# Three programs behind the rotary attention joined into one, with batch 0 a step ahead at both edges

## The reference

```
x = x + cross_attention_rotary(norm(x), ctx)      # 16 heads of 64, 2048 context rows
x = x + self_attention_0(norm(x))                 # 16 heads of 32, causal, rotary
x = x + norm(x) @ sign(weight).T
x = x + relu(cross_attention_1(norm(x), ctx) @ wo_w.T + wo_b)   # 16 heads of 32
x = x + self_attention_1(norm(x))                 # 16 heads of 64, causal
x = x + experts(norm(x))
# experts: scores = n @ Wr + br; the best 2 of 8 get softmax weights r[t, e]
# h = gelu(n @ W1[e] + b1[e]) (512 -> 2048); y = h @ W2[e] + b2[e]; out = sum_e r[t, e] * y
```

## Time and profile before

| what | value |
|---|---|
| median of 3 runs | 1226.79 us (1225.6 to 1227.8) |
| the profiled execution's own time | 1224.32 us |
| its span in the profile | 1222.2 us |
| PE busy | 1189.2 us (97%) |
| PE's weight loads busy | 954.2 us (78%) |
| DVE, ACT, POOL busy | 679.2, 531.7, 216.4 us |
| second cross-attention, first query projection to end | about 600 to 762 us |
| self-attention 1 | 762 to 840 us |
| experts | 840 to 1218 us |

### The profile page before, as it was taken

How to read it: one execution, slowest core, us unless ns; L and a number is a source line. 1 busy time by engine, 2 the same in 40 slices (tenths; PEclk the granted TensorE clock), 3 DMA queues, 4 the chain that set the end, 5 groups by cost and what they waited for, 6 DMA issues and landing times. The chain is left out here.

```text
span 1222.2 us, 23053 instructions
## 1 busy us (share of the span) xinstructions
PE 1189.2 (97%) x9712; PEld 954.2 (78%) x9712; DVE 679.2 (56%) x1210; ACT 531.7 (44%) x897; POOL 216.4 (18%) x178
## 2 busy tenths in 40 slices
PE   7999999999999999999899999997999999999998
PEld 6788888888788888865456676864989999999997
DVE  4654544545464534365788873044665665665662
ACT  5432333332333332214389994153644544444441
POOL 2243333434333433350000000010000000000000
PEclk9999999999999999999999999898999999999999
DMA  7210101010100020326313323301544554454440
GB/s 295 69 53 1 65 2 53 1 49 5 36 19 1 27 70 2 131 86 242 136 73 139 139 75 138 134 1 38 204 177 171 205 202 164 184 206 184 166 165 18
DMA packets 28157, 126.01 MB, mean 103 GB/s; under 512 B 2715, under 2 KB 2971, under 8 KB 17572
## 3 DMA queue, kind: packets, MB, share of 16 engines
q1 hardware_dynamic: 28068, 124.74, 27.2%
HBM read 124.20 MB, written 0.52 MB: 102 GB/s over the span
## 5 line engine op out<-in xcount | busy, mean ns | idle before, releaser
L566 POOL TENSOR_TENSOR norm_both<-norm_both,prob 128x512 f32<-128x512 f32 x118 | 154.8, 1312 | 149.2 <-DVE prob L358 141.8
L57 PE MATMUL mo_h_ps<-mo_x_hi,mo_w_hi 128*128 128x256 f32 x512 | 146.7, 286 | 2.1 <-DVE mo_x_lo L1800 2.1
L495 ACT ACTIVATE prob<-u_ps 128x512 f32<-128x512 f32 x128 | 66.1, 606 | 186.4 <-PE u_ps L668 186.4
L58 PE MATMUL mo_h_ps<-mo_x_lo,mo_w_hi 128*128 128x256 f32 x512 | 146.4, 286 | 0.0
L59 PE MATMUL mo_h_ps<-mo_x_hi,mo_w_lo 128*128 128x256 f32 x512 | 146.3, 286 | 0.0
L341 DVE TENSOR_TENSOR turned<-k_ps,tabs 128x512 f32<-128x512 f32 x32 | 22.1, 690 | 195.9 <-PE k_ps L59 195.9
L1754 DVE TENSOR_TENSOR mo_w_lo<-w_raw,mo_w_hi 128x2048 fp32r<-128x2048 f32 x32 | 73.3, 2292 | 73.8 <-ACT mo_w_hi L1703 73.8
L57 PE MATMUL k_ps<-ctx_hi,wk_hi 128*128 128x512 f32 x256 | 104.2, 407 | 0.0
L57 PE MATMUL u_ps<-wv_hi,ctx_hi 128*128 128x512 f32 x256 | 103.1, 403 | 0.8 <-ACT prob L495 0.8
L57 PEld LDWEIGHTS mo_h_ps<-mo_x_hi,mo_w_hi 128*128 128x128 f32 x512 | 99.8, 195 | 3.7 <-DVE mo_x_lo L1800 2.5
L484 ACT ACTIVATE vals<-u_ps 128x512 f32<-128x512 f32 x64 | 38.2, 597 | 145.8 <-PE u_ps L59 145.8
(11 more groups left out here) (264 smaller groups left out, 2297.6 us busy)
## 6 DMA issues: line engine op xcount, KB each, us to landing
w_raw<-in_w SPq DMA_DIRECT2D x64, 1024.0 KB, 6.3
ctx_raw<-in_ctx_rows SPq DMA_DIRECT2D x8, 1024.0 KB, 5.7
x_k<-in_ctx_T SPq DMA_DIRECT2D x8, 1024.0 KB, 7.0
x_val<-in_ctx_heads SPq DMA_DIRECT2D x8, 1024.0 KB, 4.9
tabs<-in_rot_tabs SPq DMA_DIRECT2D x8, 512.0 KB, 4.2
vals<-in_wq_rows SPq DMA_DIRECT2D x4, 512.0 KB, 8.0
...
x_mask<-in_mask SPq DMA_DIRECT2D x2, 1024.0 KB, 9.0
```

Source lines behind the costliest of these rows:

```text
L57: pe.matmul(out, w_hi, x_hi, start=start, stop=False)
L58: pe.matmul(out, w_hi, x_lo, start=False, stop=False)
L495: act.activation(prob[:, t % 2, i, :], u_ps[:, i, :], ACT.Exp).then_inc(s["exped"], 1)
L566: ins = pool.tensor_tensor(to, to, src, ALU.add)
```

## The change

`middle`, `self_attention` and `experts` become one function `latents` with one block; PSUM keeps its two groups of four banks, `bk[0]` and `bk[1]`, through all stages. The norms behind the second cross-attention and behind self-attention 1 are made for one batch at a time:

- `add(0)` and `moments(6, 0)` move to DVE's step t = 35 and `centred(6, 0)` to t = 36; ACT takes the root with its table load at t = 35; PE transposes batch 0 at t = 37.
- `project_cols1` works on one batch: four groups (queries and keys, batch 0 and 1) of 32 fp32 matmuls of 128 columns. The first half of the first group stands ahead of `project(1, (KD - 1,))`, the second half behind it, ahead of the transposes of batch 1.
- At the second edge the transposes of batch 0 stand ahead of the last two slices of `project_out1(1, ...)`.
- `hidden(0, 0)` is replaced by `hidden_plain`: for each batch 16 fp32 matmuls of 128 columns on the raw weights, so that unit needs no rounding (`high1(0, 0)` and `low1(0, 0)` are gone).
- `high1(0, 1)`, `high2(0, 0)`, `low1(0, 1)` and `low2(0, 0)` move ahead of the edge, into self-attention 1. For this `w2_lo` is placed elsewhere, off the output weights of that attention.
- SP fetches units 0 and 1 behind `x["y"]`, and unit 2 only after all of `hidden_plain` (`mo["h_mm"]` at 4), since that reads the raw place which unit 2 takes.

The other helpers are carried over with new names.

```diff
-    middle(nc, I, env)
-    self_attention(nc, I, env)
-    experts(nc, I, env)
+    latents(nc, I, env)
...
+        def held(m, b):
+
+            return bk[1 - (m ^ b)][:, 2 * m:2 * m + 2, :]
...
+            sp.wait_ge(x["y"], NB)
+            for U in range(2):
+                for raw, name, got in ((env["w1_raw"], "w1", env["w1_in"]), (env["w2_raw"], "w2", env["w2_in"])):
+                    sp.dma_start(raw[:, U, :, :], I[name][U * P:(U + 1) * P, :]
+                                 .rearrange("p (k n) -> p k n", k=4)).then_inc(got[U], 16)
...
+            sp.wait_ge(mo["h_mm"], NP)
+            for j in (2, 3):
+                load(0, j)
+            with sp.Fori(1, E) as e:
+                for j in range(NU):
+                    load(e, j)
...
+            def turn_norm(j, b, side, bank):
+                    ins = pe.transpose(bk[side][:, bank, k * P:(k + 1) * P], normed[:, b, k * P:(k + 1) * P], ident[:])
...
+            def project_cols1(m, b, ns):
+
+                pe.wait_ge(s["T_out"], 7 + b)
+                for n in ns:
+                    for k in range(KD):
+                        ins = pe.matmul(held(m, b)[:, n // 4, (n % 4) * P:(n % 4 + 1) * P],
+                                        (wq1, wk1)[m][:, k, n * P:(n + 1) * P], normed_T[:, k, b * P:(b + 1) * P],
+                                        start=(k == 0), stop=(k == KD - 1))
+                    if n % 4 == 3:
+                        ins.then_inc(a1["qkT"], 1)
...
+                pe.wait_ge(a1["qkT_out"], 6 + 2 * b)
...
+            def hidden_plain(b, ns):
+
+                pe.wait_ge(s1[0], 16)
+                pe.wait_ge(s["T_out"], 9 + b)
+                for n in ns:
+                    for k in range(KD):
+                        ins = pe.matmul(h_ps[:, n // 2, (n % 2) * TOK + b * P:(n % 2) * TOK + (b + 1) * P],
+                                        w1_raw[:, 0, k, n * P:(n + 1) * P], normed_T[:, k, b * P:(b + 1) * P],
+                                        start=(k == 0), stop=(k == KD - 1))
+                    if b == 1:
+                        ins.then_inc(mo["h_mm"], 1)
...
+                pe.wait_ge(mo["x_lo"], b + 1)
...
+                if t == NST + LAG - 2:
+                    turn_norm(6, 0, 0, 0)
                 if t == NST + LAG - 1:
                     project(1, range(KD - 1))
+            pe.wait_ge(w_in1, 16 * 3)
+            project_cols1(0, 0, range(4))
             project(1, (KD - 1,))
+            project_cols1(0, 0, range(4, KA1))
+            turn_norm(7, 1, 1, 2)
+            project_cols1(1, 0, range(KA1))
+            project_cols1(0, 1, range(KA1))
+            project_cols1(1, 1, range(KA1))
+            scores1(0)
...
+            project_out1(1, range(6))
+            turn_norm(8, 0, 1, 2)
+            project_out1(1, (6, 7))
+            hidden_plain(0, range(3))
+            turn_norm(9, 1, 1, 3)
+            hidden_plain(0, (3,))
+            hidden_plain(1, range(NP))
+            logits(0)
+            logits(1)
+            hidden(0, 1, first=True)
+            output(0, 0, 0, first=True)
+            hidden(0, 2)
+            turn_weights()
+            output(0, 1, 0, first=True)
+            hidden(0, 3)
...
+                if t == NST + 3:
+                    root(6, 0)
+            keep_cols1(0, 0, 0)
+            root(7, 1)
+            keep_cols1(0, 0, 1)
+            keep_norm(7, 1, 1, 2)
+            for m, b in ((1, 0), (0, 1), (1, 1)):
+                for u in range(2):
+                    keep_cols1(m, b, u)
...
+                keep_values1(1, m)
+            act.sem_inc(mo["w1_hi"], 1)
+            high1(0, 1, True)
+            high2(0, 0, True)
+            keep_out1(0)
+            keep_out1(1)
+            root(8, 0)
+            keep_norm(8, 0, 1, 2)
+            high_x(0)
+            root(9, 1)
+            keep_norm(9, 1, 1, 3)
...
+            def high_x(b):
+                act.wait_ge(s["T"], 9 + b)
+                act.activation(x_hi[:, :, b * P:(b + 1) * P], bk[1][:, 2 + b, :].rearrange("p (k t) -> p k t", k=KD),
+                               ACT.Copy).then_inc(mo["x_hi"], 1)
...
+                if t == NST + 3:
+                    add(0)
...
-                if t == NST + LAG - 1:
-                    add(0)
+                if t == NST + 3:
+                    moments(6, 0)
+                if t == NST + 4:
+                    centred(6, 0)
             add(1)
...
+            keep_out1(0)
+            keep_out1(1)
+            dve.sem_inc(mo["h_lo"], 2)
+            dve.sem_inc(mo["added"], 1)
+            dve.sem_inc(mo["w1_lo"], 1)
             step(dve.memset(r_cur[:], 0.0))
             step(dve.memset(b1_cur[:], 0.0))
             low1(0, 1)
             low2(0, 0)
             bias(0, 0, True)
...
+            add1(0)
+            moments(8, 0)
+            centred(8, 0)
+            low_x(0)
+            add1(1)
+            moments(9, 1)
+            centred(9, 1)
+            low_x(1)
```

880 lines of the change are left out of this document (376 added, 504 removed).

## The result

The changed kernel takes **1209.27 us** (median of 4 runs, 1209.12 to 1212.42), the kernel before 1227.3 us beside it: a ratio of 0.9859, interval 0.9842 to 0.9876. Against the 1226.79 us shown ahead it saves 17.5 us where I forecast 12.5. Three later sets of runs of the same two kernels gave 0.9855, 0.9866 and 0.9856.

The account below looks back on a forecast made before the run. PE, busy 97% of the span, was taken as the bound, its idle time, slow clock or work to be saved. 5.4 + 7.7 - 0.6 = 12.5 us off 1226.8 gave 1214.3 us, range 1211.4 to 1219 us.

Parts of the forecast that it names:

- Pace of the records: Plain fp32 matmuls of 128 columns, projections and first unit: 0.119 us each over 320 records, between 0.109 and 0.195 us.
- twice the columns at the same distance says that up to there the weight load sets the pace: Pricing step: 128-column transposes and 256-column fp32r matmuls both about 0.12 us apart, so the load sets the pace.
- First edge: From the last widening of the cross-attention to the first score matmul: 38.3 us become 32.9 us, 5.4 us saved.
- the wait at t = 37: PE's wait ahead of batch 0's transposes, behind ACT's root and copies: 0.3 us, between 0 and 1.5 us.
- Second edge: From the end of the attention's output layer to the logits: 16.7 us become 9.0 us, 7.7 us saved.
- Expert 0: Behind the logits: unit 2's late fetch delays rounding by 4.1 us; PE loses 0.6 us at the routing transposes, between 0 and 4.
- the slow clock behind the logits I leave as it is: Clock of 0.95 over 33 us behind the logits, about 1.6 us lost, taken as unchanged.
- From profile to median: Whole kernel: the median was taken to lie 2.5 us above the profiled execution, turning 1211.8 into 1214.3 us.
- loads don't overlap: Rival, slower: 0.195 us a record, 320 records cost 24.3 us more, the change loses 11.8 us, 1238.6 us; chance 0.04.
- The covers are thin: Rival: records 0.128 us apart, waits at t = 37 and both norms at upper ends; saving 8 us, 1219 us; chance 0.11.
- stalls move: Rival, no change: waits of the same length return inside the attention, say at `weigh1`; within 2.5 us of before; chance 0.03.
- Expert 0 gives it back: Rival: unit 2's full fetch delay of 4.1 us reaches `turn_weights`; saving 9 us, 1217.7 us; chance 0.10.

Follow-up runs that it names:

- the halved columns: The change with its query and key projections in matmuls of 64 columns instead of 128, 512 records instead of 256: 1238.91 us.
- its waits overfilled: The kernel before, PE's waits at both edges filled with 7, 10 and 4 matmuls of 512 columns whose results nobody reads: 1230.53 us.
- the split unit: The change with the plain first unit as three fp32r matmuls per batch on rounded inputs, 96 matmuls instead of 64: 1218.30 us.
- the joined edges: Two kernels, each the change with both norms' transposes together behind the whole output layer: at the first edge 1215.60 us, at the second 1212.27 us.

## Why the prediction was wrong, step by step

The mechanism was right: both edges were waits of PE, the stagger hides them, and the sign and the places came as told. The sizes were off by 5.0 us in all, and all to one side. Two terms of the sum carry most of it: the price of a record (0.119 us, measured 0.1116) and the step from profile to median (2.5 us for both kernels, measured 0.15 us for the change).

- **Pace of the records: failed.** I took 0.119 us and it is 0.1116. The 256 records of the projections gave 28.6 instead of 30.5 us: 1.9 us. The 64 of the first unit gave 2.8 + 4.7 = 7.5 instead of 7.6 us: the pace would save 0.5 us there too, but the stretch of 40 records holds 0.2 us more than 40 times the pace, and the one of 24 has its modelled end in it. The step that failed is "twice the columns at the same distance says that up to there the weight load sets the pace". The load does set it, but its floor is 0.111 us, as the halved columns show. The transposes of the earlier trace rows stand at 0.119 us, but a group of four alone takes 0.44 us (769.83 to 770.27), 0.110 us each. So the 0.119 us was not the time of a load.
- **First edge: 8.0 us instead of 5.4.** From widening to scores 8.67 us less, against 0.5 us of transposes and 0.19 us of waiting now ahead of it. 1.9 us of the miss is the pace. The other 0.7 us are small terms that I had each a little high: the last slice (0.86 instead of 1.1), the transposes, the wait at t = 37 (0.19 instead of 0.3) and the modelled end of the widening. Every cover held: the norm of batch 1 and the copies cost nothing.
- **Second edge: 8.2 us instead of 7.7.** The 0.5 us are 0.16 us at the output layer (12.12 + 1.72 = 13.84 us from start to start, where 14.00 has a modelled end), 0.26 us of waiting instead of 0.4, and 0.1 us each in the transposes and the records. The moved roundings cost nothing, as said.
- **Expert 0: no loss instead of 0.6.** The chain was right: the fetch behind the plain unit, ACT's rounding of unit 2 at 846.57 us, 4.9 us behind the logits, and DVE late at `turn_weights`. The price was double (1.25 us), and it is covered by the half clock behind the logits, or covers it. The step that failed is "the slow clock behind the logits I leave as it is". It isn't a constant: the change shows it in two of its four traces, and the stretch lasts 21.0 to 21.1 us either way. Without both losses it can be shorter: the trace of before with its waits overfilled has full clock and no wait there, and takes 19.58 us.
- **From profile to median: failed.** I added "the median lies 2.5 us above it" as if it belonged to any kernel. 1.2 us of it are half clock at the very edges that the change removes (39.6 instead of 38.8 and 31.15 instead of 30.74 us in the other traces of before). The change's own median lies 0.15 us above its profiled run, which holds one half-clock stretch near 618 us that the profile of before lacks.

Together: 12.5 + 2.6 (first edge) + 0.5 + 0.6 + 0.2 (the rest of the span) + 1.2 (half clock at the edges) = 17.6 us, against 17.5 measured. The pace is about 2 us of the first two.

Of the rivals, *loads don't overlap* is out: 0.111 us a record, with loads of 0.19 us each. So the Trainium skill's sentence (TensorE: Matmul & The Clock Gate, Part 3, The mechanism), that a load overlaps only where the row groups differ, does not hold for these full tiles. *The covers are thin* and *stalls move* did not come. *Expert 0 gives it back* named the right place and not the size. My range left out that side: its lower end took the dip behind the logits and the new waits, but kept the pace of 0.119 us, although 0.109 us stood in the text as the lower bound. With that bound (3.2 us over 320 records) the range would have held the time. It also had no term for the runs of before that lose more to half clock than its profile.

What stays open: why half clock falls between 590 and 625 us in some executions and not in others, where the split unit's runs lost time beyond its edge, and how the gain that the joined edges keep is shared among the single block, the plain unit and the clock.
